# Attention of sequence 0 from raw tokens with centred matrices, and an opening placed anew

## The reference, cut to what matters

```python
x = embeddings
x = x + attention(layernorm(x), W_Q, W_K, W_V)      # causal softmax, one head
x = x + moe(layernorm(x), ...)                      # top 4 of 32 experts, and a shared one
x = x + rwkv_block(layernorm(x), ...)               # time mixing and channel mixing
x = x + moe(layernorm(x), ...)                      # the same weights again

def layernorm(x): return (x - mean(x)) / sqrt(var(x) + 1e-5)       # over the features
def attention(h, W_Q, W_K, W_V):
    Q, K, V = h @ W_Q, h @ W_K, h @ W_V
    scores = where(causal, Q @ K.T / sqrt(128), -inf)
    return softmax(scores) @ V
```

## Time and profile before

| | |
|---|---|
| time, median of 3 runs | 797.8 us (797.49 to 798.25) |
| the profiled execution | 797.2 us, its span 795.5 us |
| TensorE busy | 788.2 us, 3793 matmuls |
| VectorE busy | 642.7 us |
| GpSimd busy | 625.3 us |
| ScalarE busy | 564.2 us |

### The profile page before, as it was taken

How to read it: one execution, slowest core, us unless ns; L and a number is a source line. 1 busy time by engine, 2 the same in 40 slices (tenths; PEclk the granted TensorE clock), 3 DMA queues, 4 the chain that set the end, 5 groups by cost and what they waited for, 6 DMA issues and landing times.

```text
span 795.5 us, 12665 instructions
## 1 busy us (share of the span) xinstructions
PE 788.2 (99%) x3793; PEld 606.1 (76%) x3793; DVE 642.7 (81%) x1531; ACT 564.2 (71%) x1032; POOL 625.3 (79%) x489
## 2 busy tenths in 40 slices
PE   8999999999999999999999999999999999999998
PEld 5688887777777776777778777787777778788786
DVE  5867766897997987987898867889788799687686
ACT  4587796867858767789676876759676775677554
POOL 7596788758668678688986898777886778967986
PEclk9999999999999999999999999999999999999999
DMA  9353434343245242452526425264443424335552
GB/s 323 83 131 77 93 82 111 76 90 90 55 106 120 58 120 53 110 133 55 121 54 137 106 60 134 50 146 97 100 116 82 108 67 109 97 70 117 122 131 69
DMA packets 49332, 80.73 MB, mean 101 GB/s; under 512 B 3280, under 2 KB 14544, under 8 KB 48880
## 3 DMA queue, kind: packets, MB, share of 16 engines
q1 hardware_dynamic: 48976, 79.72, 41.9%
q10 hardware_dynamic: 288, 0.20, 0.1%
HBM read 75.19 MB, written 4.72 MB: 100 GB/s over the span
## 4 chain that ended last, share of the span: by engine, by line
PE 98%; DMA 0%; DVE 0%; POOL 0%; ACT 0%; issue 0%; DVEq 0%; POOLq 0%
PE py L1010 10%; PE pb L982 8%; PE pa L982 8%; PE pa L986 8%; PE pb L986 8%; PE pb L983 8%; PE pa L983 8%; PE py L1015 5%; PE py L1017 5%; PE py L1016 5%; PE pu L1247 4%; PE pq L1204 2%; PE pu L1113 2%; PE pv L1089 2%; PE pu L947 1%; PE pu L1103 1%
## 5 line engine op out<-in xcount | busy, mean ns | idle before, releaser
L579 POOL TENSOR_TENSOR m_h<-m_v,m_wb 128x512 f32<-128x512 f32 x254 | 362.2, 1436 | 103.8 <-DVE m_v L1373 49.0
L715 ACT ACTIVATE m_th<-pa 128x512 f32<-128x512 f32 x222 | 131.7, 594 | 103.4 <-PE pa L986 101.6
L1373 DVE TENSOR_TENSOR m_v<-m_th,pb 128x512 f32<-128x512 f32 x208 | 140.8, 678 | 33.3 <-ACT m_th L715 19.0
L982 PE MATMUL pa<-m_xh,w1h 128*128 128x512 f32 x272 | 139.3, 512 | 0.0
L412 DVE TENSOR_TENSOR m_hl<-m_h,m_hh 128x512 fp32r<-128x512 f32 x121 | 110.2, 910 | 33.5 <-ACT m_hh L878 33.2
L878 ACT ACTIVATE m_hh<-m_h 128x512 fp32r<-128x512 f32 x183 | 114.6, 626 | 15.4 <-POOL m_h L579 13.7
L982 PE MATMUL pb<-m_xh,w3h 128*128 128x512 f32 x272 | 115.6, 425 | 0.0
L986 PE MATMUL pa<-m_xl,w1h 128*128 128x512 f32 x272 | 107.2, 394 | 0.3 <-POOL m_xl L600 0.3
L986 PE MATMUL pb<-m_xl,w3h 128*128 128x512 f32 x272 | 107.0, 393 | 0.0
L983 PE MATMUL pa<-m_xh,w1l 128*128 128x512 f32 x272 | 106.5, 391 | 0.0
L983 PE MATMUL pb<-m_xh,w3l 128*128 128x512 f32 x272 | 106.4, 391 | 0.0
(11 more groups left out here) (282 smaller groups left out, 1660.7 us busy)
## 6 DMA issues: line engine op xcount, KB each, us to landing
m_wb<-w_scratch SPq DMA_DIRECT2D x126, 512.0 KB, 6.5
x_sb<-in_x SPq DMA_DIRECT2D x8, 256.0 KB, 6.8
m_wb<-in_w SPq DMA_DIRECT2D x2, 1024.0 KB, 7.5
x_out<-x_sb SPq DMA_DIRECT2D x7, 256.0 KB, 6.8
u_scratch<-t_u SPq DMA_DIRECT2D x6, 256.0 KB, 2.9
t_u<-u_scratch SPq DMA_DIRECT2D x6, 256.0 KB, 2.8
f_kk<-in_w SPq DMA_DIRECT2D x1, 1024.0 KB, 10.5
w_scratch<-r_wT SPq DMA_DIRECT2D x16, 64.0 KB, 1.5
```

The costliest lines, as they stand in the source:

```text
L579: pool.tensor_tensor(hidden(g, p), gated(g, p), m_wb[:, p % (GRING * GP), :], ALU.mult).then_inc(sig["m_h"], 1)
L715: ins = act.activation(m_th[:, p % 2, :], pa[p % 2][:, :], ACT.Silu)
L982: pe.matmul(ps[:, :], high[:, p, :], xh, start=True, stop=False)
L1373: dve.tensor_tensor(gated(g, p), m_th[:, r, :], pb[r][:, :], ALU.mult).then_inc(sig["m_v"], 1)
```

## The change

For sequence 0 the raw tokens are transposed as soon as they are there (new semaphore a_rtr), copied as a_xr (in a_p's place), and used for G and V. The matrices are centred instead: VectorE makes `center` = ident - 1/128 (in a_pT's place), TensorE multiplies it by qk_m and by am[2], and ScalarE copies both. The factor of a query's row comes in as the scale of the exponential and, on VectorE, as a factor on the negated maximum; the factor of a value's row is the scale of the copy of V, now one copy for each tile. The keys are still the normalised a_xT. Their reciprocal deviations have a buffer of their own (a_rq). V of sequence 0 goes to pb[0] instead of pu. The decay exponential and the copy of G move ahead of ScalarE's slots, behind an exponential of one column that comes first.

All slot tuples, NATIVE, LOW_ON_POOL, LOW_LATE, TANH and FILL are written anew. Of the order in the opening: VectorE's row maximum of the last piece of sequence 0 moves from slot 6 to slot 10 (the cast of w3 keeps slot 9), the statistics of sequence 1 from slot 3 to 12, the cast of w2 from 17 to 21; GpSimd's rsqrt for sequence 1 comes behind three low quarters instead of two.

```diff
-FILL = (7, 9, 0, 2, 5, 2, 0, 2, 0, 0, 0, 0)
+FILL = (6, 0, 1, 2, 2, 0, 1, 5, 1, 0, 0, 0, 0, 0, 0)
...
+        a_rq = sb("a_rq", [P, T])
...
+        a_xr, center = a_p, a_pT[:, 0:P]
...
         def _(act):
             act.dma_start(am[:, :, :], att_mats).then_inc(sig["in_am"], 16)
             act.dma_start(vec[:, :], vecs).then_inc(sig["in_vec"], 16)
+            act.wait_ge(sig["c_pool"], 6)
+            act.activation(a_sum[:, 0:1], minus_half[:, 0:1], ACT.Exp)
+            act.wait_ge(sig["c_qkm_ps"], 1)
+            act.activation(qk_m[:, :], pv[:, 0:D], ACT.Identity, scale=SCALE).then_inc(sig["c_qkm"], 1)
+            act.wait_ge(sig["a_rtr"], 1)
+            act.activation(a_xr[:, :], pu[:, :], ACT.Copy).then_inc(sig["a_xr"], 1)
+            act.wait_ge(sig["c_qkm_ps"], 2)
+            act.activation(qk_m[:, :], pv[:, D:2 * D], ACT.Copy).then_inc(sig["c_qkm"], 1)
+            act.activation(am[:, 2, :], pb[1][:, 0:D], ACT.Copy).then_inc(sig["c_qkm"], 1)
             act.wait_ge(sig["in_vec"], 16)
             act.activation(decay[:, :], vec[:, DECAY:DECAY + 1], ACT.Exp).then_inc(sig["c_dec0"], 1)
-            act.wait_ge(sig["c_qkm_ps"], 1)
-            act.activation(qk_m[:, :], pv[:, 0:D], ACT.Identity, scale=SCALE).then_inc(sig["c_qkm"], 1)
+            act.wait_ge(sig["a_gps"], 1)
+            act.activation(a_g[:, :], pv[:, :], ACT.Copy).then_inc(sig["a_g"], 1)
...
-                    act.activation(wide(a_v[:, :, :]), pu[:, :], ACT.Copy).then_inc(sig["a_v"], 1)
-                if slot == (4, 17, 32, 30, 38, 33, 36, 37)[n]:
+                    if n == 0:
+                        act.wait_ge(sig["a_rstd"], 1)
+                        for t in range(T):
+                            ins = act.activation(a_v[:, t, :], pb[0][:, P * t:P * (t + 1)], ACT.Identity,
+                                                 scale=a_rq[:, t:t + 1])
+                        ins.then_inc(sig["a_v"], 1)
+                    else:
+                        act.activation(wide(a_v[:, :, :]), pu[:, :], ACT.Copy).then_inc(sig["a_v"], 1)
...
-                                         bias=a_nm[:, t:t + 1], accum_out=a_sum[:, t:t + 1])
+                                         bias=a_nm[:, t:t + 1], scale=1.0 if n else a_rq[:, t:t + 1],
+                                         accum_out=a_sum[:, t:t + 1])
...
-            pe.wait_ge(sig["c_pool"], 13)
-            pe.wait_ge(sig["in_am"], 16)
-            pe.matmul(pv[:, 0:D], am[:, 0, :], am[:, 1, :], start=True, stop=True).then_inc(sig["c_qkm_ps"], 1)
-            keep_clock(FILL[1])
-
...
+            pe.wait_ge(sig["in_am"], 16)
+            pe.matmul(pv[:, 0:D], am[:, 0, :], am[:, 1, :], start=True, stop=True).then_inc(sig["c_qkm_ps"], 1)
+            pe.wait_ge(sig["c_pool"], 13)
+            pe.wait_ge(sig["in_x0"], 16)
+            turn(pu, chunk(0), "a_rtr")
+            keep_clock(FILL[1])
+            pe.wait_ge(sig["c_center"], 1)
+            pe.wait_ge(sig["c_qkm"], 1)
+            pe.matmul(pv[:, D:2 * D], center, qk_m[:, :], start=True, stop=True)
+            pe.matmul(pb[1][:, 0:D], center, am[:, 2, :], start=True, stop=True).then_inc(sig["c_qkm_ps"], 1)
+            keep_clock(FILL[12])
+            pe.wait_ge(sig["a_xr"], 1)
+            pe.wait_ge(sig["c_qkm"], 2)
+            pe.matmul(pv[:, :], qk_m[:, :], a_xr[:, :], start=True, stop=True).then_inc(sig["a_gps"], 1)
+            keep_clock(FILL[13])
...
+            dve.wait_ge(sig["c_pool"], 9)
+            dve.tensor_scalar(center, ident[:, :], -1.0 / D, None, ALU.add).then_inc(sig["c_center"], 1)
...
             def att_step(n, slot):
-                if slot == (1, 3, 7, 2, 2, 11, 8, 11)[n]:
+                if slot == (2, 12, 9, 4, 2, 12, 11, 13)[n]:
...
-                if slot == (6, 28, 41, 41, 42, 42, 41, 41)[n]:
+                if slot == (10, 36, 44, 39, 42, 42, 41, 42)[n]:
                     row_max(n, 2, (3,), (0,))
...
+                if n > 0:
+                    ins.then_inc(sig["a_nm"], 1)
+                    return
+                ins.then_inc(sig["a_mx"], 1)
+                dve.wait_ge(sig["a_mx"], i + 1)
+                for t in tiles:
+                    ins = dve.tensor_scalar(a_nm[:, t:t + 1], a_nm[:, t:t + 1], a_rq[:, t:t + 1], None, ALU.mult)
                 ins.then_inc(sig["a_nm"], 1)
```

More of the change, by code:

```diff
@@ L64 @@
 LOW_ON_POOL = (
[16 rows of a table removed]
+    (0, 2, 3, 5, 9, 12),
+    (3, 4, 5, 7, 8, 9, 12, 14, 15, 16),
+    (11, 14),
+    (2, 5, 6, 10, 12, 13),
+    (1, 6, 7, 9, 10, 11, 12, 13, 14, 15),
+    (2, 4, 5, 6, 10, 11, 14),
+    (6, 10, 11, 16),
+    (3, 8, 12),
+    (1, 6, 10, 11, 12, 15),
+    (0, 1, 4, 6, 7, 8, 9, 12, 14),
+    (5, 10, 12, 15, 16),
+    (3, 6, 11, 12),
+    (2, 12, 14),
+    (1, 3, 4, 14),
+    (2, 11, 13, 14),
+    (1, 16),
 )
@@ L89 @@
 LOW_LATE = (
[L90 to L105, removed]
+    (1, 2, 3, 7, 10, 11, 14, 15),
+    (0, 1, 4, 5, 10, 11, 12, 13, 14, 15),
+    (3, 7, 15),
+    (0, 5, 6, 7, 10, 12, 13),
+    (5, 12, 14, 15),
+    (4, 13, 14, 15),
+    (7, 8, 16),
+    (0, 6, 9, 16),
+    (1, 8, 15, 16),
+    (14,),
+    (1, 5, 8, 10, 13),
+    (1, 2, 3, 6, 10, 11, 14, 16),
+    (3, 7, 9),
+    (9, 16),
+    (0, 3, 4, 10, 12),
+    (3, 4, 6, 7, 9, 12, 13, 14, 15),
 )
 TANH = (
-    (0, 1, 4, 8, 10, 11, 12),
-    (),
+    (0, 1, 8, 9, 10, 11, 12, 15),
+    (7,),
     (12, 13),
@@ L1052, in att_step @@
                     if n_chunk is not None and n_chunk_in_pv:
                         pe.wait_ge(sig["m_x"], n_chunk)
-                    pe.matmul(pv[:, :], qk_m[:, :], a_xT[:, 0:S], start=True, stop=True).then_inc(sig["a_gps"], 1)
-                if slot == (5, 19, 22, 25, 32, 29, 33, 36)[n]:
+                    if n > 0:
+                        pe.matmul(pv[:, :], qk_m[:, :], a_xT[:, 0:S], start=True, stop=True).then_inc(sig["a_gps"], 1)
+                if slot == (0, 14, 21, 21, 37, 30, 33, 30)[n]:
+                    pe.wait_ge(sig["c_qkm"], 3)
+                    ps, xT = (pu, a_xT) if n else (pb[0], a_xr)
@@ L1057, in att_step @@
                     for t in range(T):
-                        ins = pe.matmul(pu[:, P * t:P * (t + 1)], a_xT[:, P * t:P * (t + 1)], am[:, 2, :],
+                        ins = pe.matmul(ps[:, P * t:P * (t + 1)], xT[:, P * t:P * (t + 1)], am[:, 2, :],
                                         start=True, stop=True)
                     ins.then_inc(sig["a_vps"], 1)
-                if slot == (5, 21, 30, 30, 33, 33, 37, 36)[n]:
+                if slot == (0, 22, 21, 32, 34, 33, 35, 33)[n]:
+                    if n == 0:
+                        keep_clock(FILL[14])
+                    pe.wait_ge(sig["a_xT"], n + 1)
@@ L1096, in probs @@
                     keep_clock(FILL[5 + i])
+                if n == 0 and i == 0:
+                    pe.wait_ge(sig["a_v"], 1)
                 pe.wait_ge(sig["a_exp"], 3 * n + i + 1)
@@ L1170, in spread_step @@
             def spread_step(slot):
-                if slot == (37,)[0]:
+                if slot == (36,)[0]:
                     pe.wait_ge(sig["r_wT"], 1)
@@ L1461, in pro_step @@
             def pro_step(q, slot, cmix):
-                if slot == (15,)[0] and q == 0:
+                if slot == (18,)[0] and q == 0:
                     dve.wait_ge(sig["a_add"], 2)
@@ L1575, in fold_step @@
             def fold_step(slot):
-                if slot == (3,)[0]:
+                if slot == (14,)[0]:
                     dve.wait_ge(sig["in_vec"], 16)
```

314 lines of the change are left out of this document (158 added, 156 removed), and 35 rows, old and new, of tables (LOW_ON_POOL, NATIVE).

## The result

The changed kernel takes 804.04 us (median of 4 runs, 802.55 to 805.74), the kernel before 798.01 on the same chip (797.49 to 798.25). The ratio is 1.0080, with an interval of 1.0067 to 1.0092: slower by 6.4 us, where 1.4 us faster was forecast. The profiled execution took 805.74 us with a span of 804.0.

A forecast was written before the change was run, and what follows sets the result against it. Behind about 37 us the time is the sum of TensorE's instructions, before that a chain of latencies. Counts -1.0, opening -0.4 and slots +0 make -1.4: 797.8 - 1.4 = 796.4 us, range 794.4 to 798.6.

The forecast's parts named there:

- Each group's moves leave the work as it is: Re-placed slots in the loop's groups: the work is unchanged, only small waits come or go; taken as zero.
- Counts, -1.0: MoE loop: native down-product units go from 89 to 83, and six conversions give back 1.0 us of TensorE time.
- The 0.17 for a conversion: MoE down-products: a split one takes TensorE 0.69 us, a native one 0.86, so each conversion gives back 0.17.
- I price these at nothing: MoE loop: added copies, low halves and gate steps (some 4 us on ScalarE, 15 us on VectorE) cost no time.
- The rival of VectorE's head of the line: Late groups: gates come behind waiting low halves on VectorE and TensorE stands; eight waits of 0.4 give 799.6; chance 0.10.
- Opening, -0.4: Opening, sequences 0 and 1: the MoE loop starts 0.4 us sooner; bounds a loss of 0.5 and a gain of 1.4.
- first scores: Attention of sequence 0 on TensorE: scores start at 9.8 us instead of 11.49, 1.7 sooner.
- the last tile's maximum behind the cast of w3: VectorE in sequence 0: the last tile's row maximum starts at 13.8 us, behind that cast, instead of 14.3.
- the turn of sequence 1: Opening: TensorE's transposes of sequence 1 start at 19.3 us; the prediction is wrong if they come at 18.5 or 20.
- Clock, chance 0.05: Rival in the opening: the kernel is slower by the clock, as fillers fall from 27 to 18; chance 0.05.
- Slots, zero between -1.5 and +3: Moved slots outside the opening: small waits taken away or added, taken as zero us, between -1.5 and +3.

The follow-up runs named there:

- the two profiles of after: The changed kernel, unedited, profiled in its first measurement (median 804.04 us, profiled execution 805.74 us) and once more (802.63 us, one run).
- the two kernels with the new order: The kernel before and the changed kernel, buffers reordered so every TensorE operand starts at a multiple of 128 bytes: 796.22 us and 797.97 us.

## Why the prediction was wrong

**What bounds the kernel** was read rightly (TensorE's instructions one behind the other), but the reading "the time is the sum of TensorE's instructions" was used with durations that were taken as fixed. The failed step is "Each group's moves leave the work as it is. They can take away or add small waits." It holds for instructions and not for addresses: the new buffer a_rq was not priced at all, because it issues no instruction. It makes the passes 0.0039 us longer. For the 2,199 passes of after's MoE that would be 8.6 us; shown by the run with the buffer last are 4.7, and 6.9 by the unused bytes in the kernel before. The traces have two reasons for less. Steps of over 0.26 us don't grow, as told above. And waits shrink when TensorE is slower: with the buffer last there are 27 long steps, 5.1 us in all, in the two profiles of after only 8 and 5, 2.5 and 1.2 us.

**Counts, -1.0.** The 0.17 for a conversion is TensorE's side alone, and as that it holds: from the start of the last pass before a down-product to that of the third behind it the kernel before takes 1.374 us (medians) where it is split and 1.544 where it is native. The step that failed is "I price these at nothing": the room for a low half more in a slot wasn't there in the old order (11 us, half of it the gate behind a waiting low half), and in the new order the same list is worth -2.6. The rival of VectorE's head of the line was a true mechanism, with a chance of 0.10, but for after itself the new places of the low halves had answered it.

**Opening, -0.4.** Right in size: the loop starts 0.54 to 0.58 us sooner (36.54 and 36.50 against 37.08). Right in its steps: first scores 9.62 (forecast 9.8), the last tile's maximum behind the cast of w3, the turn of sequence 1 at 19.01 (19.3). Only in the first profile of after, with its slow start, did the turn come at 20.59, behind the 20 that the prediction named as a sign against it. Wrong in that the 0.4 reaches the end: by itself this opening gives 1.0012.

**Clock, chance 0.05.** In the first profile of after the loop starts 1.63 us later than in the second, with G at 2.05 us in place of 1.10; that this is the clock is inferred from the length of such matmuls. The column of the granted clock reads 1.00 for 6 to 10 us of that profile, but the trace has no record of the clock for this time: its first record, of 1.00, begins at 10.76 us there and between 4.29 and 7.07 us in the sixteen other profiles, and the column shows 1.00 where no record is. G started at 7.38, ahead of it. In the others with this opening G took 1.10; by medians it is not the cause.

**Slots, zero between -1.5 and +3.** With the new buffer last the ratio is 1.0021, 1.7 us above the kernel before, where counts and opening should have given 1.4 to 1.6 below: some 3.2 us of new waits, a little outside the bound that I had. In that profile there are 27 long steps, 5.1 us in all, against 16 and 2.0 us, and groups 0, 2, 4, 5, 6 and 15 are longer than before by 0.3 to 0.85 us each. Which slots or lists make them is open; I didn't undo them one group at a time.

**The range** ended at 798.6. Without the moved buffers 799.23 would still have been outside it; the forecast had the wrong sign for this part too, since it set waits that could be taken away against waits that could be added as if both were as likely, in a loop whose trace had hardly any left to take.

## What to carry to other kernels

Before a change is priced by its instructions, look at what it does to the addresses behind it: here 32 unused bytes in the middle of the allocation cost 6.9 us, where the whole edit was to give 1.4. Keep small buffers last and the moving operands of the busiest products on a multiple of 128 bytes, the fastest place of the three tried here (0.2298 us a pass, against 0.2323 and 0.2337), and test any edit that allocates against the old kernel with the same number of unused bytes. And where a hand-written order has no gap on its bounding engine, its lists and slots are one thing: turning one of them alone cost 11 us one way and 2.6 the other.

## What the runs showed of the hardware that I had not expected

The pace of TensorE's passes of 512 columns depends on where the buffers start: 0.2298 us with the moving operands on a multiple of 128 bytes, 0.2323 at 64 behind one, 0.2337 at 32 behind one, with no instruction different between the first and the last. The weights lay 64 bytes behind a multiple of 128 in all but the two kernels with the new order, where the passes took 0.2291; whether the weights do that, or the moving operands' place modulo 256, no run separates. The third passes of the down-products started 0.0045 us later, too, when only the up-products' operands had moved modulo 128, which that rule can't explain.

Operations of VectorE and GpSimd took longer side by side, both ways: GpSimd's power over 4 columns took 1.92 us in place of 1.01 beside a cast on VectorE, VectorE's scalings 2.05 in place of 1.12 beside a low part on GpSimd, and the cast 2.23 in place of 1.22 beside a low quarter. In all three the longer one started second, at 20.04 behind 19.88, 22.00 behind 21.93 and 16.36 behind 16.22, and the first took its usual time (1.22, 1.26 and 1.29 us). By what they get in each other's way no run shows.

The time from which the trace has a granted clock of 1.00, and the matmuls their shorter length, is not fixed in the opening: with the same program it lay before G (record from 7.07 us, G at 7.16 in 1.10 us) in one execution and behind it (record from 10.76, G at 7.38 in 2.05 us) in another.
